# Edge loops of a graph network kernel: turned one-hots from a broadcast load and a VectorE compare, longer rings, gather indices two blocks ahead

## What is computed

```
e[s,d,h]  = leaky_relu(a_src[s,h] + a_dst[d,h], 0.2)
p         = exp(e - max over the edges into d)
out[d,h,:] = sum(p * feature[s,h,:]) / sum(p)
```

## Time and profile before

| what | value |
|---|---|
| timed runs | 4284.76 us median of 3 (4278.98 to 4286.46) |
| profiled execution | span 4872.5 us, 63960 instructions; no other time is listed for it |
| PE busy | 3544.1 us, 73% of the span |
| DVE busy | 2671.7 us, 55% |
| ACT busy | 1621.1 us, 33% |
| POOL busy | 1291.4 us, 27% |
| first edge loop | about 82 to 965 us of the span |
| second edge loop | about 1290 to 2160 us of the span |

### The profile page before, as it was taken

The page is one execution under the profiler, slowest core; times in us unless marked ns, Lnnn a source line. Parts: engine busy times, 40 slices in busy tenths (PEclk is TensorE's granted clock), DMA queues, the critical chain, the costliest instruction groups (busy, mean ns, idle before and its releaser), DMA issues. The chain is left out here.

```text
span 4872.5 us, 63960 instructions
## 1 busy us (share of the span) xinstructions
PE 3544.1 (73%) x22446; PEld 2944.2 (60%) x22446; DVE 2671.7 (55%) x6836; ACT 1621.1 (33%) x4188; POOL 1291.4 (27%) x1348
## 2 busy tenths in 40 slices
PE   3365556667345455576988999997999879969796
PEld 3244444456334333465775888887457879968795
DVE  5465556754445555557865888887212533344444
ACT  1133333311122232334553666665111122321131
POOL 6454454245354455400000000000000022210063
PEclk8676667778667677788999999998999989989898
DMA  5233333233433333344500000003455431135324
GB/s 152 78 101 98 101 108 90 82 102 98 110 91 101 98 109 107 92 109 131 135 9 5 1 1 1 1 1 76 110 126 139 154 107 37 37 84 136 131 71 123
DMA packets 178027, 419.54 MB, mean 86 GB/s; under 512 B 58688, under 2 KB 103410, under 8 KB 177216
## 3 DMA queue, kind: packets, MB, share of 16 engines
q1 hardware_dynamic: 116800, 251.73, 18.6%
q0 software_dynamic: 60928, 164.04, 11.7%
HBM read 331.25 MB, written 84.36 MB: 85 GB/s over the span
## 5 line engine op out<-in xcount | busy, mean ns | idle before, releaser
L836 POOL DMA_INDIRECT sb<-features,sb x850 | 832.8, 980 | 785.9 <-DVE sb L901 540.6
L2054 PE MATMUL ps<-sb 128*128 128x125 f32 x5184 | 635.6, 279 | 71.2 <-DVE sb L2118 70.1
L2054 PEld LDWEIGHTS ps<-sb 128*128 128x128 f32 x5184 | 595.0, 192 | 111.8 <-DVE sb L2118 110.5
L3447 ACT ACTIVATE sb<-ps,sb 128x128 f32<-128x128 f32 x784 | 220.1, 376 | 572.5 <-PE ps L3373 500.4
L1194 PE MATMUL ps<-sb 128*125 128x128 bf16 x850 | 117.1, 286 | 395.0 <-PEq L1192 188.1
L2085 ACT ACTIVATE sb<-ps 128x125 f32<-128x125 f32 x1296 | 330.0, 272 | 223.7 <-PE ps L2054 194.9
L3373 PE MATMUL ps<-sb 128*128 128x128 f32 x3136 | 393.2, 282 | 12.7 <-DVE sb L3418 8.5
L1205 PE MATMUL ps<-sb 128*125 128x260 f32 x1700 | 394.1, 391 | 9.9 <-PEq L1203 6.2
L545 DVE TENSOR_SCALAR sb<-sb 128x782 bf16<-128x782 f16 x425 | 188.2, 493 | 373.8 <-PE ps L619 162.8
L3387 PE MATMUL ps<-sb 128*128 x1568 | 373.5, 385 | 19.5 <-issue 10.3
L3373 PEld LDWEIGHTS ps<-sb 128*128 128x128 f32 x3136 | 377.7, 198 | 16.3 <-DVE sb L3418 11.0
(11 more groups left out here) (357 smaller groups left out, 5493.9 us busy)
## 6 DMA issues: line engine op xcount, KB each, us to landing
sb<-adj SPq DMA_DIRECT2D x125, 683.6 KB
neg<-sb SPq DMA_DIRECT2D x25, 683.6 KB
adj<-sb SPq DMA_DIRECT2D x25, 683.6 KB
sb<-neg SPq DMA_DIRECT2D x25, 683.6 KB
sb<-rows_y SPq DMA_DIRECT2D x30, 560.0 KB
sb<-in_L_ffn_W SPq DMA_DIRECT2D x16, 1024.0 KB
sb<-features,sb POOLq DMA_INDIRECT x850
sb<-adj SPq DMA_DIRECT2D x125, 79.3 KB
```

Source lines behind the costliest of these rows:

```text
L836: e.indirect_dma_start(hgs[i % 4][:, w, :], None, k.HR, indirect(ids[i % 3][:, w:w + 1])).then_inc(*hg_in[i % 4].by(16))
L2054: return e.matmul(sums(n, g)[:, 0, :], V[:, y, (4, 0, 5, 1, 2, 3)[g], :], self.old_h(n)[:, y, :], start=False, stop=y == 1, skip_group_che ...
L3447: m = e.activation(hts[n % 2][:, c, :], hidden(n, c), ACT.Gelu, bias=cons[n % 4][:, c:c + 1])
```

## The change

- `EdgeTable` also writes the destinations alone, as f16 less 1562, to a DRAM table `D16` of 17 per row.
- In the loops SP loads for each block the 128 x 17 destinations (4352 bytes) into all 125 partitions (`destinations`). DVE compares them with each partition's own node number (`turned`), which gives `DT` directly, now ordered [node, edge row, 17]. `turn` and `copy_turned` are gone; the weights of `expand` are slices `DT[:, :, w]` with a step of 17 elements.
- `expand` goes to bank 0 instead of bank 4, `rel` and `shares` move from PSUM bank 0 to SBUF, the columns get a third bank (1).
- The ring of adjacency one-hots has eight tiles instead of four. `widen` has one f32 tile instead of two and stands earlier in ACT's order.
- `indices` is called for block i+2 instead of i+1.

```diff
+MID = 1562
+HOTS = 8
...
     def sync_store(self, e):
+        flat16 = k.D16.rearrange("r c -> (r c)")
+        e.wait_ge(*self.d16_set.at(1))
+        e.dma_start(flat16[0:E].rearrange("(p c) -> p c", p=P), self.d16[:, :]).then_inc(*self.d16_out.by(16))
+        e.dma_start(flat16[E:ROWE * W].rearrange("(p c) -> p c", p=5), self.pad16[:, :]).then_inc(*self.d16_out.by(16))
...
+        e.memset(self.pad16[:, :], -1.0 - MID)
+        e.tensor_scalar(self.d16[:, :], self.de[:, :], -float(MID), None, ALU.add).then_inc(*self.d16_set.by())
...
-        self.hots = [k.sb(ctx, [128, FOLD + 2], bf16) for _ in range(4)]
+        self.hots = [k.sb(ctx, [128, FOLD + 2], bf16) for _ in range(HOTS)]
...
-            e.wait_ge(*self.used.at(W * self.order(t) + max(w - 3, 0)))
-            e.tensor_scalar(self.hots[w % 4][:, 0:FOLD], self.ioF[:, :], eg[:, w, 1:2], eg[:, w, 2:3],
+            e.wait_ge(*self.used.at(W * self.order(t) + max(w - HOTS + 1, 0)))
+            e.tensor_scalar(self.hots[w % HOTS][:, 0:FOLD], self.ioF[:, :], eg[:, w, 1:2], eg[:, w, 2:3],
...
-        return (5, 7)[g % 2]
+        return (5, 7, 1)[g % 3]
...
-        wides = [k.sb(ctx, [128, W, P]) for _ in range(2)]
-        DT = k.sb(ctx, [P, W, 128], bf16)
+        wide = k.sb(ctx, [128, W, P])
+        DT, drow = k.sb(ctx, [P, 128, W], bf16), k.sb(ctx, [P, 128 * W], f16)
+        node16 = k.sb(ctx, [P, T])
-        shares = k.PS[:, 0, 0:4 * W].rearrange("p (w h) -> p w h", h=4)
-        rel = k.PS[:, 0, 4 * W:5 * W]
+        shares = k.sb(ctx, [128, W, 4])[:, :, :]
+        rel = k.sb(ctx, [128, W])[:, :]
...
+                def destinations(b):
+                    row = nc.values_load(
+                        k.at[0:1, b:b + 1], engines=[mybir.EngineType.SP], min_val=0, max_val=ROWE - 128,
+                        skip_runtime_bounds_check_because="the edges before a block by W, less a half")
+                    if b >= 1:
+                        e.wait_ge(*turned_made.at(b))
+                    e.dma_start(drow[:, :], broadcast_row(k.D16[bass.ds(row, 128), :].rearrange("r c -> (r c)"),
+                                                          P)).then_inc(*row_in.by(16))
...
                 for b in range(T):
                     x = b % 2
+                    if b >= 1:
+                        destinations(b)
                     e.wait_ge(*sl_made.at(b + 1))
...
+                def turned(b):
+                    e.wait_ge(*row_in.at(16 * (b + 1)))
+                    if b >= 1:
+                        e.wait_ge(*expanded.at(b))
+                    e.tensor_scalar(DT[:, :, :].rearrange("p e w -> p (e w)"), drow[:, :], node16[:, b:b + 1], None,
+                                    ALU.is_equal).then_inc(*turned_made.by())
+                    e.wait_ge(*turned_made.now())
+                    e.sem_inc(turned_token.sem, 1)
...
                 def hot(b):
-                    if b == 1:
-                        e.wait_ge(*widened.at(1))
                     if b >= 2:
-                        e.wait_ge(*dt_turned.at(5 * (b - 1)))
                         e.wait_ge(*widened.at(b - 1))
...
                 e.wait_ge(*numbered.at(2))
                 indices(0)
+                indices(1)
+                e.tensor_scalar(node16[:, :], part[0:P, :], -float(MID), None, ALU.add).then_inc(*vs.by())
+                e.wait_ge(*vs.now())
                 for i in range(T):
...
-                    if i + 1 < T:
-                        indices(i + 1)
+                    if i + 2 < T:
+                        indices(i + 2)
                     if 0 <= i - 2 < T:
                         logits(i - 2)
+                    if i >= 1:
+                        turned(i - 1)
                     if 0 <= i - 3 < T:
                         close.vector_second(e, i - 3)
...
-                def copy_turned(b):
-                    if b >= 1:
-                        e.wait_ge(*expanded.at(b))
-                    for g in range(5):
-                        n = min(4, W - 4 * g)
-                        e.wait_ge(*dt_turned.at(5 * b + g + 1))
-                        e.activation(DT[:, 4 * g:4 * g + n, :].rearrange("p w c -> p (w c)"),
-                                     k.bank((5 * b + g) % 2, n * 128, P),
-                                     ACT.Copy).then_inc((bank_token if g < 4 else turned_token).sem, 1)
...
                 def widen(b):
-                    if b >= 2:
-                        e.wait_ge(*summed.at(b - 1))
+                    if b >= 1:
+                        e.wait_ge(*summed.at(b))
...
                 for i in range(T):
                     if i >= 2:
                         own_share(i - 2)
+                        widen(i - 2)
                     if i >= 3:
                         close.scalar(e, i - 3)
-                    if i >= 1:
-                        copy_turned(i - 1)
                     if i >= 2:
                         exp_logits(i - 2)
-                    if i >= 1:
-                        widen(i - 1)
...
                     for w in range(W):
-                        m = e.matmul(k.PS[:, 4, w * 27:w * 27 + 27], DT[:, w, :],
+                        m = e.matmul(k.PS[:, 0, w * 27:w * 27 + 27], DT[:, :, w],
                                      dms[u % 2][:, :, :].rearrange("p s c -> p (s c)"), start=True, stop=True)
...
-                def turn(u, times, first=False):
+                def placed():
                     e.wait_ge(dt_token.sem, 1).then_inc(dt_token.sem, -1)
-                    for g in range(5):
-                        if g >= 2 or (g == 0 and not first):
-                            e.wait_ge(bank_token.sem, 1).then_inc(bank_token.sem, -1)
-                        for x in range(min(4, W - 4 * g)):
-                            m = e.matmul(k.PS[0:P, (5 * u + g) % 2, x * 128:x * 128 + 128],
-                                         dts[u % 2][:, 4 * g + x, :], id16[:, :], start=True, stop=True)
-                        m.then_inc(*dt_turned.by(1, times))
...
                 def step(u, times, second, cols):
                     expand(u, times)
-                    turn(u + 1, times)
+                    placed()
```

More of the change, by code:

```diff
@@ L330, in __init__ @@
         self.pad, self.bad, self.full = k.sb(c, [8, 1095]), k.sb(c, [P, 2]), k.sb(c, [1, T])
[L331 to L334, removed]
+        self.d16, self.pad16 = k.sb(c, [P, 400], f16), k.sb(c, [5, 438], f16)
+        self.src_in, self.dst_in, self.next_in, self.ends_out, self.pad_out, self.rec_out, self.d16_out = (
+            k.sig(s) for s in ("src_in", "dst_in", "next_in", "ends_out", "pad_out", "rec_out", "dst16_out"))
+        self.numbered, self.gs, self.pad_set, self.next_set, self.rec_set, self.d16_set = (
+            k.sig(s) for s in ("numbered", "gstep", "pad_set", "next_set", "rec_set", "dst16_set"))
         self.floats, self.lasts, self.rows_set, self.counted, self.tallied, self.summed, self.placed, self.vs = (
@@ L369, in sync_end @@
         e.wait_ge(*self.rec_out.at(16))
+        e.wait_ge(*self.d16_out.at(32))
     def gpsimd(self, e):
@@ L510, in __init__ @@
         self.mask = k.sb(ctx, [P, N], bf16)
-        self.cols = k.sb(ctx, [P, T, P], f16)
+        self.flat = k.sb(ctx, [P, T * P + 1], f16)
+        self.cols = self.flat[:, 0:T * P].rearrange("p (t i) -> p t i", i=P)
         self.numbered, self.folded, self.used = k.sig("folds_numbered"), k.sig("folds_set"), k.sig("hot_used")
@@ L619, in tensor_products @@
                 r = e.matmul(k.PS[0:P, 2 + x, 0:392], dt[:, w, :],
-                             self.hots[w % 4][:, 392 * x:392 * x + 392], start=w == 0, stop=w == W - 1)
+                             self.hots[w % HOTS][:, 392 * x:392 * x + 392], start=w == 0, stop=w == W - 1)
             r.then_inc(*self.used.by(1, times))
@@ L625, in tensor_cols @@
         e.wait_ge(self.field_token.sem, 1).then_inc(self.field_token.sem, -1)
[L626 removed]
+        e.wait_ge(self.col_token.sem, 3)
         for g in range(7):
@@ L803, in by_edges @@
         adj = Adjacency(k, ctx, odd, id16)
+        hot_rows = adj.flat[0:ROWS, 0:8 * P].bitcast(f32)
         numbered = k.sig("numbered")
@@ L814, in by_edges @@
             k.sig(s) for s in ("self_made", "self_exp", "logit_made", "logit_exp"))
-        expanded, dt_turned, summed = k.sig("expanded"), k.sig("dt_turned"), k.sig("summed")
+        expanded, summed = k.sig("expanded"), k.sig("summed")
+        row_in, turned_made = k.sig("destinations_in"), k.sig("turned_made")
         set16, widened = k.sig("id16_set"), k.sig("widened")
-        rows_token, dm_token, turned_token, terms_token, dt_token, bank_token, wide_token, scaled_token, sum_token = (
-            k.token(s) for s in ("rows_token", "dm_token", "turned_token", "terms_token", "dt_token", "bank_token",
-                               "wide_token", "scaled_token", "sum_token"))
+        rows_token, dm_token, turned_token, terms_token, dt_token, wide_token, scaled_token, sum_token = (
```

(32 more changed lines are left out.)

12 lines of the change are left out of this document (5 added, 7 removed).

## The result

The changed kernel takes 4427.6 us (median of 4, 4415.5 to 4429.6) against 4284.5 us (4279.0 to 4286.5): ratio 1.033 [1.0317, 1.0343], **slower by 143 us**. The forecast was 4300 us, the range ended at 4350. The profiled execution took 4428.38 us with a span of 4426.1 us, so here span and time agree, which they did not before.

A forecast was written before the change was run, and what follows sets the result against it. It took DVE and POOL as level at 44 us a period in the first loop, POOL alone at 43.5 in the second. Terms 14 + 4 - 6 + 3 = +15 us on 4284.8 gave 4300 us, range 4210 to 4350.

The forecast's parts named there:

- the port's term: Both loops: two-SBUF-input L966 and L1011 beside POOL's gathers; the sum followed short row L992 and added nothing.
- The third rival: Slower by POOL's port: L966 and L1011 with SBUF operands add 56 us to POOL, 4346 us; chance 0.12.
- the rate of L545's kind: POOL's gather lengthening per DVE busy time, 29 us laid to 188 us of such work: 0.154.
- First loop, +1.2 us a period: First edge loop: 2.2 us added by `turned`, 1.0 us of turning waits removed; x 12 gives +14 us.
- SP is not late: Broadcast load of destinations on SP's queue: some 20 us of cover until the next iteration's middle, cost 0.
- Second loop, POOL alone at 43.5, +4 us in all: Second edge loop: DVE's 41.2 us hidden under POOL's 43.5 us; longer gathers from the compare cost +4 us.
- Strided weights, taken at 0 of 0 to 14: Loads of `expand`, 17 a block: hidden because DVE has other work first, 0; upper bound 14 us.
- Indices two ahead, -6 us: POOL's indices: no steady-state gain, a sooner start of either loop; -6 us, bounds 0 and -20.
- Setup, +3: Setup: one more DVE pass over 400 columns, four more clears a loop, two small transfers; +3 us.
- The inference that I called the weak point: Profile's 587.7 us excess: delayed completions under gathers, of which a timed run has almost none.
- The extreme of the first rival: Faster rival (chance 0.37) at its limit: handoff delays also in timed runs, half of L545's 373.8 us gone, 4156 us.
- The test that I named: Whole kernel: the span falls far more than the time, perhaps by 250 us, without a gain in timed runs.

The follow-up runs named there:

- e17: The kernel before, unchanged, run for a profile in set A: 4278.2 us, span 4275.4 us.
- e11: The kernel before with only `shares` and `rel` moved from PSUM to SBUF, in set A: 4397.7 us, 1.0265 of the kernel before.
- e10: The changed kernel with `shares` and `rel` back in PSUM (bank 1) and two column banks, in set A: 4326.0 us, 1.0096 of the kernel before.
- set A: Groups of runs in which the kernel before takes about 4283 us in every unprofiled run; the official comparison is of this kind.
- set B: Groups of runs in which the kernel before takes about 4855 us in every unprofiled run; the profile that the prediction read is of this kind.
- e5: The changed kernel with `shares` and `rel` back in PSUM and two column banks, in set B: 4633.3 us, 0.9538 of the kernel before.
- e9: The changed kernel with `shares` and `rel` back in PSUM and two column banks, again in set B: 4677.4 us, 0.961 of the kernel before.
- e7: The version of e5 with indices one block ahead instead of two, in set B: 4749.9 us, 0.9787 of the kernel before.
- e0: The kernel before, unchanged, profiled a second time, in set B: 4854.9 us, span 4853.7 us.

## Why the prediction was wrong

**The step that failed is the port's term, set to 0.** "My sum follows the short rows": L992, 0.23 us long, two SBUF inputs, no trace of a delay. I read DVE's idle time before it, 3.6 us, and the delay falls on POOL. Nor would POOL's rows have shown it: the 45 gathers that overlap L992 take 947 ns in the mean, in e17 as in e11. The operations that lengthen gathers here are the long ones. By my reckoning from the changed kernel's trace (each gather's time over 946 ns laid to the DVE operation that overlaps it most), 72 us of 118.8 busy belong to L997 and 61 of 245.0 to L1042: rates of 0.61 and 0.25. The third rival took 0.154, the rate of L545's kind, and so said 56 us where the runs show 97 to 115. It had the mechanism, the condition (mean over 1.0 us, here 1.16) and the sign, with a chance of 0.12. L992 was near by its operands and far by its length, and L545's kind near by neither; no row of before had both, so the upper bound should have been the operations' whole 363 us of busy time, not 0.154 of it. That this one term carried the loss past the range is seen in e10: without it the change takes 4326 us, between the forecast and the top of 4350. The Trainium skill (SBUF — State Buffer, Who interferes with whom) has the rule: DVE instructions with two SBUF inputs contend with a GpSimd instruction that reads SBUF. e11 agrees with it (1127 against 989 ns a gather), and with one of the two operands in PSUM the lengthening under these operations is gone (949 ns in e17).

**The other terms** sum to +15 in the forecast and to +43 in e10 (4326.0 - 4283.1), which has two column banks instead of the change's three.

- First loop, +1.2 us a period: measured 46.95 - 44.88 = +2.07. Busy time rose by (373.68 - 365.05) / 9 = 0.96; the rest is waiting. The hots' wait that went was 6.2 us in this loop, not 12. A new one came, for the destinations, whose cover I had put at some 20 us, with "SP is not late". SP is late: in every second block of e10 it issues the load 8 to 11 us after the compare that frees the tile, 11 to 13 us before the next compare, and all but one of the waits are in those blocks. In e10 (timeline, then the waits of the first loop):

```profile
296.06 1.00 DVE L975 TENSOR_SCALAR sb<-sb 125x2176 bf16<-125x2176 f16 x1 [2.21 <-DMA sb<-destinations]
...
DVE sb L975 <- DMA sb<-destinations: 10.3, 9, 2.2
```

- Second loop, POOL alone at 43.5, +4 us in all: POOL did bound it, at 44.16 before and 45.13 in e10; +0.97 a period makes 12 us. In this loop a gather's mean went from 997 to 1022 ns: 25 ns x 425 = 11 us. Most of that is not the new compare, which accounts for 5 us over both loops (same reckoning), near what I forecast for one. The hots lengthen gathers too: 30 us in e10 against 11 us in e17. They now run without pauses between them, which may be why; no run separates it.
- Strided weights, taken at 0 of 0 to 14: the median load is 160 ns in e10 instead of 96 in e17, and the 17 matmuls of a block take 1.19 us from first to last instead of 0.58. In e10's second loop DVE waits 16.6 us for them, where in the whole of e17 it waits 1.1:

```profile
DVE sb L1017 <- PE ps L1210: 16.6, 11, 1.8
```

  That loop is POOL's, so I take most of this as hidden; no run separates it.
- Indices two ahead, -6 us: nothing that shows in set A, inside the bounds.
- Setup, +3: the start came 0.7 us later. Between the loops 5.7 us went, and 9.9 after the second loop's last one-hots; neither was in the sum.

By loop lengths (first to last one-hots): 552.5 to 571.5 and 546.2 to 559.6, +19.0 and +13.4; with 5.7, 9.9 and 0.7 that is the 48.7 us between the spans of e17 and e10.

**The inference that I called the weak point** held in what it said and not in why. Timed runs of set A have almost none of the 587.7 us, and the periods that I worked out for them, 43.9 and 43.5 us, were 44.88 and 44.16. But the delay is no matter of profiling: profiled and timed runs agree in each set. The extreme of the first rival, "the handoff delays are in the timed runs as well", is what set B does: there the change's family gains 4 to 5% (e5, e9). Of this the indices two ahead are worth 117 us (e7 against e5). That the rest comes from the turning's handoffs, which are gone, fits the waits that go but was not shown. The test that I named, a span that falls much more than the time, came true (4872.5 to 4426.1 us), but compared two kinds of run rather than two kernels.

**Against both kernels** no version that ran beats the kernel before in set A. e10's beats the changed kernel there (4326.0 against 4422.6) and the kernel before in set B (0.954 to 0.961 of it).

## What to carry to other kernels

Beside indirect DMAs issued by GpSimd, try to keep one operand of every long two-operand VectorE operation in PSUM: a move of small tiles to SBUF that costs VectorE nothing cost this kernel 97 to 115 us. Price such sharing by an operation of the same kind *and* length, read on the engine that would be delayed, or bound it by the whole busy time. And before you read waits in a profile, see whether its span is near the timed median; if it is not, the waits may be those of another condition of the machine, and a further profile is worth more than an inference from sums.

## What the runs showed of the hardware that was not expected

- One kernel has two times, 4283 and 4855 us, constant within a group of runs, and chips of the same number appeared in both kinds. Of the 578 us between the spans of e0 and e17, 550 lie in the two loops (830.7 and 818.3 us from first to last one-hots, against 552.5 and 546.2). There it shows as waits for which the trace has no reason, as if completions arrived late while gathers run (18.87 us against at most 4.0 us in e17). What brings it about stays open. It is worth some 570 us to the kernel before (4855 - 4283) and 307 to 351 to e10's version (e5 and e9 against e10), so it can turn the verdict on a change.
- A gather that begins 0.25 us after the start of a two-SBUF-operand operation of DVE takes 2.35 us instead of 0.95. Per microsecond of busy time the bf16 operation of 2.38 us costs POOL 0.61 us and the f32 ones of 1.69 us, three in a row, 0.25; whether length, type or order makes the difference was not tried.
- Weights with a step of 17 bf16 elements: medians of 162 against 96 ns a load. The following rows are of e17 and of the changed kernel (ns min/median/max, first and last start):

```profile
L1184 PEld LDWEIGHTS ps<-sb x850: 95/96/109, 130.4 to 1541.0; 125*128 125x128 bf16 x170
```

```profile
L1210 PEld LDWEIGHTS ps<-sb x850: 138/162/174, 127.7 to 1681.6; 125*128 125x128 bf16 x170
```

- A compare of 2176 f16 elements to bf16 takes 0.80 us, where the slope of the shorter one of 782 gave 1.04.
